# An eight-block network in one kernel: the rotation table moves to the quantised stage, head sums are spread, feed-forward stages begin with the high parts

## The reference, cut to what matters

```python
x = LN(x + series(x) + down(silu(gate(x)) * up(x)))      # 1 feed-forward, F = 1248
x = LN(x + x @ W_org.T + sum_e coeff_e * x @ down_e @ up_e)  # 2 experts; coeff = softmax of mean(x) keys
x = LN(x + attention(x))         # 3 sequence length 1 over 256 "batches" of one: attn = V, so W_v W_o
x = LN(x + (silu(x @ Wg) * (x @ Wu)) @ Wd)               # 4 quantised: W = (int - zero) * scale, I = 1792
x = LN(x + conv_network(x))      # 5 convolution with prog = p ** arange(L), p complex, 4 layers of 64
x = LN(x + two_loras(x))         # 6
x = LN(x + causal_attention(x))  # 7
x = LN(x + (silu(x @ Wg) * (x @ Wu)) @ Wd)               # 8 integer weights times one scale, F = 1376
```

## Time and profile before

| | |
|---|---|
| median of 3 runs | 1472.1 us (1471.62 to 1472.14) |
| profiled execution, its time | 1473.04 us |
| profiled execution, its span | 1471.3 us |
| mean granted TensorE clock | 0.912 |
| busy: PE, DVE, ACT, POOL | 1273.6 (87%), 752.7 (51%), 426.1 (29%), 143.8 (10%) us |
| experts, value matrix (249.6 to 398.3) | 148.7 us |
| quantised stage starts | 398.4 us |
| last stage starts | 1274.0 us |

### The profile page before, as it was taken

The page is one execution under the profiler, slowest core; times in us unless marked ns, Lnnn a source line. Parts: engine busy times, 40 slices in busy tenths (PEclk is TensorE's granted clock), DMA queues, the critical chain, the costliest instruction groups (busy, mean ns, idle before and its releaser), DMA issues. The chain is left out here.

```text
span 1471.3 us, 14461 instructions
## 1 busy us (share of the span) xinstructions
PE 1273.6 (87%) x5250; PEld 830.6 (56%) x5250; DVE 752.7 (51%) x1301; ACT 426.1 (29%) x709; POOL 143.8 (10%) x208
## 2 busy tenths in 40 slices
PE   7999997759799998983565698989999999599998
PEld 4787665324378887763443244444454444388877
DVE  5223323792656555423546563877777641433254
ACT  2222111110221214210221212136666666311141
POOL 0000000490000000001111004000101113000000
PEclk9999998889899999985566699989999999899999
DMA  7110001450066630004000001000000000021000
GB/s 307 44 43 0 0 0 61 204 200 0 15 229 207 217 147 0 1 16 141 1 0 0 0 0 43 0 1 1 2 2 2 2 3 0 27 81 64 22 22 36
DMA packets 18681, 78.82 MB, mean 54 GB/s; under 512 B 3330, under 2 KB 4226, under 8 KB 16452
## 3 DMA queue, kind: packets, MB, share of 16 engines
q1 hardware_dynamic: 18628, 78.13, 14.8%
HBM read 75.76 MB, written 2.10 MB: 53 GB/s over the span
## 5 line engine op out<-in xcount | busy, mean ns | idle before, releaser
L346 PE MATMUL psum<-L_ffn_x,L_ffn_w_up 128*128 128x512 f32 x1200 | 276.7, 393 | 16.2 <-DVE L_ffn_x L475 16.2
L346 PEld LDWEIGHTS psum<-L_ffn_x,L_ffn_w_up 128*128 128x128 f32 x1200 | 228.2, 190 | 64.4 <-issue 16.6
L1756 DVE TENSOR_REDUCE mqa_top<-psum 128x1 f32<-128x512 f32 (+3 forms) x304 | 186.0, 656 | 57.5 <-PE psum L1582 37.7
L1675 ACT ACTIVATE mqa_prob<-psum 128x512 f32<-128x512 f32 x288 | 159.8, 601 | 85.9 <-PE psum L1600 84.5
L363 PE MATMUL psum<-L_ffn_wd,L_ffn_part_h 128*128 128x512 f32 x600 | 140.1, 394 | 7.1 <-DVE L_ffn_wd L298 7.0
L1600 PE MATMUL psum<-mqa_stack,mqa_keys 100*128 100x512 f32 x288 | 132.7, 475 | 4.7 <-DMA mqa_stack<-mqa_rows 3.4
L363 PEld LDWEIGHTS psum<-L_ffn_wd,L_ffn_part_h 128*128 128x128 f32 x600 | 113.0, 190 | 31.4 <-DVE L_ffn_part_h L289 7.8
L346 PE MATMUL psum<-L_attn_x,L_attn_w_up 128*128 128x512 f32 x480 | 111.3, 394 | 3.9 <-DVE L_attn_hidden L464 3.9
L1571 PE MATMUL psum<-mqa_keys,mqa_stack 96*128 96x512 f32 (+1 forms) x256 | 107.4, 439 | 2.3 <-DVE mqa_top L1756 1.0
L346 PEld LDWEIGHTS psum<-L_attn_x,L_attn_w_up 128*128 128x128 f32 x480 | 91.2, 190 | 23.8 <-issue 4.8
L464 DVE TENSOR_TENSOR L_ffn_hidden<-L_ffn_gate,psum 128x512 f32 (+1 forms) x50 | 34.3, 686 | 136.7 <-PE psum L346 136.0
(11 more groups left out here) (239 smaller groups left out, 1632.4 us busy)
## 6 DMA issues: line engine op xcount, KB each, us to landing
L_ffn_stage<-in_L_w SPq DMA_DIRECT2D x25, 768.0 KB, 6.6
L_ffn_z_int<-in_L_z SPq DMA_DIRECT2D x14, 768.0 KB, 4.4
L_ffn_s_all<-in_L_s SPq DMA_DIRECT2D x14, 768.0 KB, 6.2
lora_wo<-in_L_wo SPq DMA_DIRECT2D x8, 1024.0 KB, 4.8
L_attn_stage<-in_L_w SPq DMA_DIRECT2D x10, 512.0 KB, 3.6
L_attn_w_down<-in_L_down SPq DMA_DIRECT2D x1, 2560.0 KB, 23.9
x_feat<-in_x_feat SPq DMA_DIRECT2D x2, 1024.0 KB, 7.0
x_tok<-in_x_tok SPq DMA_DIRECT2D x1, 2048.0 KB, 18.3
```

The lines of the kernel that those rows point to most:

```text
L346: ins = nc.tensor.matmul(bank[half][:, :], w_up[:, slot, w_part, at:at + P], x[:, x_part, k, half * HALF:(half + 1) * HALF], start=k == 0 ...
L1675: nc.scalar.activation(prob[:, n % PROBS, :], score_bank[n % 3], ACT.Exp, scale=SCALE)\
L1756: nc.vector.tensor_reduce(top[:, i % 2, lo // HALF, heads[0]:heads[-1] + 1], max_bank[n % 3][:, 0:len(heads) * width] .rearrange("p (h k) ...
```

## The change

Four parts:

- **Rotation table.** GpSimd builds it in the quantised stage, after x is split, with `x_feat` (not read again until the stage's tails write it) as its scratch. Levels 7, 8 and 9 are paced: after three, two and one products it waits for the next tile's `product`. ScalarE waits for the table before it begins the down product. VectorE's preparation goes behind the tails and head sums of the expert product.
- **Head sums.** Three lie before and among the effective weight's additions, one each after tiles 2, 4 and 6, two after tile 7. The head blocks are loaded before `w_org` and `wv`.
- **Coefficients.** ScalarE takes half of the mean and half of the scaled copies.
- **Feed-forward stages** (all three): the first half of tile 0 goes pass by pass, high times high for gate and up, then x low, then weight low, each with its own wait; VectorE makes the first low x half before the low weights.

```diff
+def first_half():
+    for n, (w_part, x_part) in enumerate(PASSES):
+        if n == 0:
+            pe.wait_ge(w_hi, base["w_hi"] + 1)
+        elif n == 1:
+            pe.wait_ge(x_lo, base["x_lo"] + 1)
+        else:
+            pe.wait_ge(w_lo, base["w_lo"] + 1)
+        for which, bank, done in ((0, g_bank, gate_done), (1, u_bank, up_done)):
+            for k in range(KC):
+                at = (which * KC + k) * P
+                ins = nc.tensor.matmul(bank[0][:, :], w_up[:, 0, w_part, at:at + P],
+                                       x[:, x_part, k, 0:HALF],
+                                       start=k == 0 and n == 0, stop=k == KC - 1 and n == 2)
+            if n == 2:
+                ins.then_inc(done, 1)
...
+                    if first and slot == 0:
+                        split_x(0)
                     dve.wait_ge(w_hi, base["w_hi"] + f + 1)
...
+                    pool.wait_ge(x_lo, base["x_lo"] + 2)
+                    table.pool(pool, lambda pool, f: pool.wait_ge(product, base["product"] + 2 * f + 2))
...
+                if table is not None:
+                    act.wait_ge(table.half_ready, 1)
                 for g in range(2):
                     split_h(act, 0, g, 0)
```

```diff
                 c.rot.load(sp, a)
-                sp.dma_start(w_org[:, :, :], a["L0_org"]).then_inc(org_loaded, 16)
-                sp.dma_start(wv[:, :, :], a["L1_wv"]).then_inc(wv_loaded, 16)
                 for g in range(KV):
                     if g >= SLOTS:
                         sp.wait_ge(paired, g - SLOTS + 1)
                     sp.dma_start(wo[:, g % SLOTS, :, :], a["L1_wo"][g]).then_inc(wo_loaded[g % SLOTS], 16)
+                    if g == 1:
+                        sp.dma_start(w_org[:, :, :], a["L0_org"]).then_inc(org_loaded, 16)
+                    if g == SLOTS:
+                        sp.dma_start(wv[:, :, :], a["L1_wv"]).then_inc(wv_loaded, 16)
...
-                c.rot.pool(pool)
...
+                for k in range(2, KC):
+                    nc.scalar.activation(wide_sum[:, k - 2, :], c.x_feat[:, k, :], ACT.Copy,
+                                         accum_out=mean[:, k:k + 1]).then_inc(mean_by_act, 1)
...
+                for r in range(RC):
+                    ins = nc.scalar.activation(up_c[0:R, r, :], up[0:R, r, :], ACT.Copy,
+                                               scale=coeff[0:R, 2 * r:2 * r + 1])
+                ins.then_inc(coeff_ready, 1)
+                tail.act(act)
                 c.rot.act(act)
-                tail.act(act)
...
-                c.rot.dve(dve)
+                add_heads(0)
                 dve.wait_ge(org_loaded, 16)
                 for i in range(KC):
                     dve.wait_ge(delta_ready, i + 1)
                     nc.vector.tensor_tensor(w_eff[:, i, :], w_org[:, i, :], c.bank[i][:, :], ALU.add)\
                         .then_inc(eff_ready, 1)
+                    if i in (0, 1):
+                        add_heads(i + 1)
                 for t in range(NT):
                     tail.dve(dve, t)
+                    if t in (2, 4, 6, 7):
+                        add_heads(3 + (2, 4, 6, 7).index(t))
+                add_heads(7)
+                c.rot.dve(dve)
```

```diff
+        in_one_tile = {7: 3, 8: 2, 9: 1}
...
+            def paced(ins):
+                nonlocal ops, tile
+                then(ins)
+                ops += 1
+                if level in in_one_tile and ops % in_one_tile[level] == 0:
+                    after_tile(pool, tile)
+                    tile += 1
```

More of the change, by code:

```diff
@@ L220, in swiglu @@
 def swiglu(c, front, down=None, last=None, x_loaded=None, first_loads=None, extra_loads=None,
-           extra_dve=None, extra_pe=None, extra_act=None):
+           extra_dve=None, extra_pe=None, extra_act=None, table=None):
     nc = c.nc
@@ L332, in _ @@
                     extra_pe[0](pe)
+                def first_half():
[14 more added lines that the diff above has]
+                                ins.then_inc(done, 1)
                 def gate_and_up(f, slot, first):
+                    if first and slot == 0:
+                        first_half()
                     pe.wait_ge(w_lo, base["w_lo"] + f + 1)
-                    for half in range(2):
+                    for half in range(1 if first and slot == 0 else 0, 2):
                         if first and slot == 0:
-                            pe.wait_ge(x_lo, base["x_lo"] + half + 1)
+                            pe.wait_ge(x_lo, base["x_lo"] + 2)
                         else:
@@ L471, in _ @@
                 split_w_up(0, 0, True)
[L472 to L476 removed]
+                split_x(1)
                 split_w_up(1, 1, True)
```

85 lines of the change are left out of this document (44 added, 41 removed).

## The result

The changed kernel takes 1449.8 us (median of 4 runs, 1447.5 to 1452.1), against 1472.1 us (4 runs, 1471.6 to 1472.3) for the kernel before on the same chip: a ratio of 0.984 with a 95% interval of 0.982 to 0.986. It is faster by 22.4 us, where 29.6 were forecast. The time lies inside the range of 1437 to 1452, near its upper end.

What follows compares the result with a forecast made beforehand. TensorE was taken as the bound, except in the expert product, where GpSimd's products slow VectorE. Expert -24.4, quantised -1.9 and last stage -3.5 give -29.8 us: 1442.3 on the median, stated as 1442.5, range 1437 to 1452.

Steps and rivals of the forecast that it cites:

- The second rival: Expert tiles: VectorE stays the bound or a head block is late, 5 to 8 us more, 1449 us; chance 0.13.
- the fourth: Rival: slower than before, each split waits through all GpSimd products of its tile, 1491 us; chance 0.03.
- Expert stage, -24.4: Expert section: the value product starts at 339.1 instead of 363.5, 24.4 us sooner; bounds -26.5 and -19.5.
- the three sums in the loop: Expert tiles: head sums after tiles 2, 4 and 6 delay TensorE's transposes 0.3 us each, 0.7 in all.
- The coefficients: Before the expert product: scaled copies shared by VectorE and ScalarE save 1.7 us before the delta matmuls; the halved reduction nothing.
- Quantised start, -3.4: Quantised stage: TensorE starts 3.6 us sooner, needing only high parts; 0.2 us lost at tile 1, gain 3.4 us.
- Last stage, -3.5: Last feed-forward stage: TensorE starts once the rounded weights are there, 3.5 us sooner; bounds -2 and -3.6.
- The third rival: Feed-forward starts: the early start does nothing, tile 1 waits anyway; 5.4 us less gain, 1448 us; chance 0.12.
- The products on GpSimd, +1.5: Quantised stage: GpSimd's table products delay VectorE's weight splits, costing 1.5 us of stall; stage net -1.9, bounds -3.4 and +8.
- the free stretch: Quantised stage, tiles 2 and 3, unpaced products: delays of 1 and 2 us exceed the slack, 1.5 us of stall.
- the paced stretch: Quantised stage, paced products from level 7: splits start 3 to 4 us after the multiply, when products are nearly over.
- The first rival: Quantised stage: the products move the port's stall there, stage 8 us longer than before, put at 1456 us; chance 0.12.

Runs made afterwards that it cites:

- The two runs that undo one part each: Changed kernel with the rotation table back in the expert section: 1457.6 us; changed kernel with all eight head sums back in the expert tile loop: 1449.7 us.
- The run paced by the multiply: Kernel with GpSimd's products between weight splits, but each group starts at a tile's second multiply instead of behind a split: 1446.7 us.
- the kernel between the splits: Changed kernel with each GpSimd group of levels 7 to 9 waiting for the end of a VectorE weight split: 1445.8 us, later 1439.8 us.

## Why the prediction was right, and what was off

**What bounds the kernel: right.** Both halves of the reading stand. The expert product was bound by VectorE, which GpSimd's products held up, and is now as fast as its twin. The two runs that undo one part each show that the products were the larger cause (20.2 us without them alone, 11.0 with the sums spread alone). The second rival, VectorE still the bound of the expert tiles or a head block late, is refuted by the same figures: TensorE's tiles are 3.87 us apart and the merge waits for no sum. So is the fourth, slower than before.

**Expert stage, -24.4: measured -24.1.** The tiles are 3.9 us apart (3.81 foreseen), and the first addition of a sum beside no product costs 1.22 us. For the three sums in the loop 0.7 us stood in the sum, and they cost TensorE nothing: its tiles start 3.87 us apart in both products. That the seven tiles take 27.31 us by their residual adds against 26.67 in the value product is the last add alone, 0.6 late behind the sum of tile 6. From its start to the merge the expert product took 30.6 us, 31.4 foreseen. The merge and what follows it came to 28.9 us (311.00 to 339.91; 29.1 foreseen). The coefficients gave 0.5 us in the first profile, not 1.7; but that stretch has a low clock at its start and varies from run to run of one kernel: 36.6 to 39.0 us in the eleven profiles of kernels with the new coefficients and no table beside them, against 39.5 and 39.2 in the two with the old. The mean of the eleven, 37.5, is 1.8 us less, but three of them are at 39.0 and eight at 36.6 to 37.1, and two profiles with the old ones are few to tell how much is the coefficients' doing. The total is in part luck: in the first profile 1.2 us less from the coefficients are nearly made up by 0.8 more from the expert product and 0.2 from the merge, and by the second and third profile of the changed kernel the stage gained 26.4 and 26.3 us. `down` was there at 260.3 and the copies took 1.69 us on VectorE and 2.56 on ScalarE, so ScalarE's four ended last, as assumed (2.0 and 2.3).

**Quantised start, -3.4: measured -3.2 to -3.5. Last stage, -3.5: measured -3.3.** The early start alone gives 6.7 us and leaving it out costs as much in the traces. The third rival, an early start that does nothing, is refuted in both stages. (Its price was short: 5.4 us is the stage's net 1.9 and the last stage's 3.5; without the two starts 3.4 and 3.5 are missing, 6.9.) TensorE starts 4.25 us after the first instruction; 4.2 were named as the sign.

**The products on GpSimd, +1.5: measured +6.1, 6.7 and 6.5.** This is the term that was mis-sized, and most of the difference between 29.6 and 22.4 us. The mechanism was named: each of the four operations of a split can wait for one product, and the loop through the load passes it on. The step that failed is "In the free stretch (tiles 2 and 3) delays of 1 and 2 us push it over, and I count 1.5 us of stall." The delays there were 4.85 us in one split (9.75 against 4.9) and 3.9 in the next (8.8), because the products lie end to end beside the four operations, and an operation takes until one of them is over. Four waits of a microsecond each were in the text, and the sum counted one or two. Not all of it reaches TensorE: of these 8.75 us the multiplies lost 4.5, and the slack of the loop and the place of the splits in it took up the rest. "In the paced stretch it rights itself" holds in part: at 445.12 the split does come 4.2 us behind the multiply and takes 1.84 us, but the next two are hit again (2.39 us at 455.74, 3.56 at 466.75), and 1.6 of the 6.1 us are lost from there on. The splits came 3.5 to 4.2 us behind the multiply, as foreseen, but the products were not nearly over by then: they begin 0.83 us after the multiply does, and the third of level 9 takes 4.62 us, not 3.8, so they end 4.4 and 5.5 us behind it. The run paced by the multiply shows the same: a group that starts at the multiply is safe only while it ends before the split, and neither a pair of 1024 columns nor one product of 2048 does. One of the prediction's own signs of being wrong came true with this, the 10.88 us per tile that rise while GpSimd works (13.6 and 12.6 in tiles 3 and 4), and TensorE waits 3.2 us for the multiply, where under 2 was named. The first rival had this with its mechanism at a chance of 0.12, but with too high a price: the stage 8 us longer than before, where it came out 2.9 us longer (6.1 less 3.2). It is a case between the forecast and that rival.

The Trainium skill (SBUF — State Buffer, "Summary: rules for kernel authors") says that with two SBUF inputs on VectorE and GpSimd reading SBUF the second to issue is blocked until the first is done. The trace agrees for VectorE (the 0.68 us operation at 421.65 ends at 424.03, just over half a microsecond after the product that began before it), and in the other direction (the product at 323.60 of the kernel with the table in the expert stage takes 5.38 us instead of 4.62). Taken literally, four operations each blocked by one product is the count that should have been made for each of the two splits.

**The rest.** The 2.3 us of the last down product, and the half microsecond each of the first stage and of the stretch between the down product and the last stage were not in the sum. The 2.3 us are no part of the change: they come and go between executions of one kernel. Sum of the first profile: +0.5 - 24.1 - 3.2 + 6.1 + 0.2 + 0.5 - 3.3 + 2.3 = -21.0 us, its span's difference. Against the forecast of -29.8 that is 8.8 us: 4.6 from the products, 2.3 from the clock in the last product, 1.2 from the first stage, the down product and the middle, and 0.7 from terms that were each off by 0.2 or 0.3.

**What stays open.** Why the clock falls in some executions and not in others after the same 3.4 us of idle time isn't settled; after the 3.64 us in the quantised stage it fell every time. The time that the kernel between the splits gains over the changed one was 2.9 us in one group and 9.5 in another, around the 6.1 to 6.7 us that the traces show. A placement of the products that also leaves level 6 and narrower clear of the splits was not tried.

## What to carry to other kernels

The same work on GpSimd beside VectorE's operations on two SBUF operands cost nothing or 6 us by its place: tie it to the end of those operations (a split's last one), not to an event after which they come soon. Count such contention per operation: four short operations beside four long ones waited four times, and in a loop with 0.6 us of slack per turn half of it showed. And look at what a stage's twin without the contention takes: it gave the new pace of the expert tiles (3.87 us in both), and the gain of the stage to within 2 us.

## What the runs showed of the hardware that was not expected

**The other direction of the blocking.** GpSimd's products stretch as well: 2.75 and 2.22 us instead of 1.89 for 1024 columns, 5.38 instead of 4.62 for a subtraction of 2048, when VectorE's operations get in between.

**A lock of the two engines.** With groups started by the multiply the split's first operation took 2.80, 3.25, 3.24, 2.44, 2.49 and 3.49 us in six tiles running, and the loop turned in 11.1 to 12.0 us, without drifting out of the collision until the products were over.

**The clock after a pause.** The start of the quantised stage's down product had a low granted clock after a pause of 3.64 us in twelve profiles of twelve, and a full one after 1.07 us in two of two. After the last stage's 3.40 us it was low in six of twelve.

**The spread of one kernel.** Two profiles of the changed kernel have spans of 1450.3 and 1441.9 us with the same instructions. Of the 8.4 us, 3.6 lie in the convolution's stretch (windows of 150.0 and 146.4 us at granted clocks of 0.63 and 0.65), 2.2 in the coefficients and the delta matmuls, and 2.3 in the last down product. The kernel before ran from 1469.7 to 1479.8 us in the three groups. One profile of a kernel can so be several microseconds off from its own next one, in stretches where the granted clock is not full throughout; a stretch at full clock, as tile 2 to the last multiply, repeats to a hundredth (119.57 us in eight profiles of six kernels).
